# Two halves of the batches for the last experts and the last 64 steps, residuals read from PSUM by VectorE, and new operation lists in a two-layer block kernel

## What is computed

```
x = x + ga * attn0(layernorm(x) * (1 + ca) + sa)      # layer 0: gated delta rule, step by step over time
x = x + gb * ffn0(layernorm(x) * (1 + cb) + sb)       # layer 0: 8 experts, top 2, plus its own input
x = x + ga * attn1(layernorm(x) * (1 + ca) + sa)      # layer 1: state space layer, chunks of 64 steps
x = x + gb * ffn1(layernorm(x) * (1 + cb) + sb)       # layer 1: 128 -> 512, butterfly, gelu, butterfly, -> 128

def ffn0(xt):                                         # all experts computed, weighted by w
    h  = silu(einsum('nd,edh->enh', xt, we1) + be1)
    eo = einsum('enh,ehd->end', h, we2) + be2
    return xt + einsum('ne,end->nd', w, eo)           # w: softmax over the top 2 of 8 logits

def attn1(x):
    xi, w = x @ in_proj                               # xi: causal convolution of 4 taps -> xh;  A = w * w_base
    y = ssd(xh, A, chunk=64)                          # decays, running sums, state carried to the next chunk
    return y @ out_proj.T
```

## Time and profile before

| | us |
|---|---|
| median of 3 runs | 543.15 |
| lowest and highest | 539.29, 543.17 |
| the profiled execution | 537.53 |
| its span, first to last instruction | 535.6 |
| PE, ACT, DVE, POOL busy in the span | 434.6, 368.9, 329.5, 173.2 |

### The profile page before, as it was taken

How to read it: one execution, slowest core, us unless ns; L and a number is a source line. 1 busy time by engine, 2 the same in 40 slices (tenths; PEclk the granted TensorE clock), 3 DMA queues, 4 the chain that set the end, 5 groups by cost and what they waited for, 6 DMA issues and landing times.

```text
span 535.6 us, 6713 instructions
## 1 busy us (share of the span) xinstructions
PE 434.6 (81%) x2060; PEld 290.7 (54%) x2060; DVE 329.5 (62%) x741; ACT 368.9 (69%) x624; POOL 173.2 (32%) x240
## 2 busy tenths in 40 slices
PE   4767876669878688999888999999899999965075
PEld 2546845447556466567655656666566565641021
DVE  0525954786899963979989995499231194211910
ACT  5889777894966838788439774765997877925233
POOL 1150940574347761077940305233002100030001
PEclk9889997999999899999999999999999999995579
DMA  8739665024800068002074000000000000000000
GB/s 197 246 83 260 203 267 158 1 52 108 215 4 2 1 158 219 3 0 61 19 182 118 1 1 21 0 1 1 1 0 21 0 1 2 1 20 0 0 1 20
DMA packets 34323, 35.46 MB, mean 66 GB/s; under 512 B 12776, under 2 KB 30320, under 8 KB 34032
## 3 DMA queue, kind: packets, MB, share of 16 engines
q1 hardware_dynamic: 34000, 30.84, 21.9%
q10 hardware_dynamic: 288, 4.19, 2.0%
HBM read 13.78 MB, written 1.05 MB: 28 GB/s over the span
## 4 chain that ended last, share of the span: by engine, by line
PE 32%; ACT 8%; POOL 5%; DVE 4%; issue 3%; POOLq 0%; DVEq 0%
PE psS L776 9%; PE psF L761 9%; PE psM L812 3%; PE psM L819 3%; PE psB L718 2%; PE psM L596 2%; PE psB L605 1%; ACT hS L1329 1%; POOL QS L3019 1%; ACT L1286 1%; ACT hid L1479 1%; POOL A L3006 1%; PE psM L799 1%; PE psM L805 1%; ACT L1284 1%
## 5 line engine op out<-in xcount | busy, mean ns | idle before, releaser
L776 PEld LDWEIGHTS psS<-we2s,hid 128*128 128x128 f32 x1024 | 129.3, 193 | 43.7 <-issue 34.9
L761 PE MATMUL psF<-h,we1s 128*128 128x512 f32 (+1 forms) x320 | 134.8, 523 | 21.2 <-ACT hid L1479 15.3
L776 PE MATMUL psS<-we2s,hid 128*128 128x128 f32 x1024 | 131.8, 277 | 8.7 <-DVE acc L2063 5.5
L1479 ACT ACTIVATE hid<-psF,col 128x512 f32<-128x512 f32 (+1 forms) x160 | 93.1, 599 | 59.8 <-PE psF L761 51.2
L761 PEld LDWEIGHTS psF<-h,we1s 128*128 128x128 f32 x320 | 54.8, 194 | 61.7 <-ACT hid L1479 33.0
L3019 POOL TENSOR_TENSOR QS<-H,qn 128x256 f32<-128x256 f32 x64 | 51.4, 814 | 83.7 <-DVE H L2051 71.0
L2063 DVE SCALAR_TENSOR_TENSOR acc<-psS,gate,acc 128x128 f32<-128x128 f32 x128 | 40.4, 340 | 59.2 <-PE psS L776 47.8
L1286 ACT ACT_TABLE_LOAD x44 | 56.5, 1283 | 1.5 <-PEq L3326 0.7
L2030 DVE TENSOR_TENSOR psT<-wrep,H 128x360 f32<-128x360 f32 x64 | 46.1, 720 | 12.8 <-DMA wrep<-XX 11.1
L2051 DVE TENSOR_TENSOR_SCAN H<-A,psT 128x320 f32<-128x320 f32 x64 | 52.3, 817 | 1.7 <-issue 0.3
L1284 ACT ACT_TABLE_LOAD x30 | 38.5, 1283 | 0.5
(11 more groups left out here) (194 smaller groups left out, 641.8 us busy)
## 6 DMA issues: line engine op xcount, KB each, us to landing
wrep<-XX SPq DMA_DIRECT2D x72, 160.0 KB, 3.3
krep<-kn SPq DMA_DIRECT2D x64, 128.0 KB, 2.5
hid<-fold_mats_dram SPq DMA_DIRECT2D x22, 256.0 KB, 4.4
we1s<-we_dram ACTq DMA_DIRECT2D x1, 2048.0 KB, 7.8
we2s<-we_dram ACTq DMA_DIRECT2D x1, 2048.0 KB, 12.5
outT_dram<-x SPq DMA_DIRECT2D x4, 256.0 KB, 2.6
M<-mats_dram SPq DMA_DIRECT2D x1, 576.0 KB, 5.1
x<-xT_dram SPq DMA_DIRECT2D x2, 256.0 KB, 6.8
```

The lines of the kernel that those rows point to most:

```text
L761: mm(bank[name][:, 0:ncols(w)], we1s[:, e, k * P:(k + 1) * P], h2[w % 2][:, 0:ncols(w)], start=True, stop=True).then_inc(s_hid_mm, 1)
L776: last = mm(bank[name][:, t * P:(t + 1) * P], hid[n % 2][:, k, t * P:(t + 1) * P], we2s[:, e, k, :], start=(k == 0), stop=(k == HT - 1))
L1479: nc.scalar.activation(hid[x_ % 2][:, k, 0:c], psF[n % 2][:, 0:c], ACT.Silu, bias=pc("be1", HT * e + k)).then_inc(s_hid_done, 1)
```

## The change

1. The experts of the last window run as two units: `EU` lists (window, first batch, last batch), units 4 and 5 being batches 0 to 3 and 4 to 7 of window 4. `first`, `hidden`, `second`, `mix` and `experts_back` take a unit; in units 4 and 5 they work on 256 columns and two tiles of tokens.
2. The last block of 64 steps of the second layer runs as two units of four batches: `SU`, units 3 and 4. They have tiles of their own (`last4`, `hS1`, `EE1`, laid over `krep`, which the recurrence has left by then), and banks of their own for unit 4 (S0, S1, F0, F1). Their `ssd_last`, `ssd_carry`, `ssd_factors` and `ssd_state` are left out, since no block follows.
3. The residuals: DVE adds the product times the gate to x directly from PSUM, one operation of 64 (or 32) columns for each batch (`experts_residual`, `ssd_residual`, `ffn_residual`). `experts_branch`, `ssd_branch`, `ffn_out` and POOL's `ssd_residual`, `ffn_gate` and `ffn_residual` go. POOL adds the experts' own input times the gate to x (`experts_gate`, `experts_skip`) as soon as it is normalized, and the feed-forward's bias times the gate (`ffn_shift`, with `out_bias` once on DVE) after the centring.
4. The list of every engine is placed anew, SP's with it.

```diff
+EU = [(w, 0, NB) for w in range(W - 1)] + [(W - 1, 0, NB // 2), (W - 1, NB // 2, NB)]
+SU = [(v, 0, NB) for v in range(NV - 1)] + [(NV - 1, 0, NB // 2), (NV - 1, NB // 2, NB)]
+LASTS = [u for u in range(len(SU)) if SU[u][0] == NV - 1]
...
@@ sync
             spread_solved(1)
+            spread_keys(3)
             spread_keys(2)
-            spread_keys(3)
             spread_solved(2)
             spread_solved(3)
-            spread_keys(5)
             spread_keys(4)
             spread_solved(4)
             spread_solved(5)
+            spread_keys(5)
+            spread_keys(7)
             spread_keys(6)
             spread_solved(6)
-            spread_keys(7)
             spread_solved(7)
...
@@ tensor
+            def first(u, e, k):
+                w, a, b = EU[u]
+                n = HT * (EXPERTS * u + e) + k
...
+                mm(bank[name][:, 0:(b - a) * TWS[w]], we1s[:, e, k * P:(k + 1) * P], h2[w % 2][:, a * TWS[w]:b * TWS[w]], start=True,
                    stop=True).then_inc(s_hid_mm, 1)
...
+            first(5, 7, 0)
+            first(5, 7, 1)
+            variance(("ssd", 3))
+            first(5, 7, 2)
+            first(5, 7, 3)
+            second(5, 6, 0)
+            second(5, 6, 1)
+            second(5, 7, 0)
+            second(5, 7, 1)
+            experts_back(5)
+            ssd_steps(3)
+            center(("ssd", 4))
+            ssd_in(3)
+            variance(("ssd", 4))
+            fill(2)
+            ssd_steps(4)
+            ssd_in(4)
+            ssd_out(3)
+            ssd_out(4)
+            center(("ffn", 3))
+            center(("ffn", 4))
+            variance(("ffn", 3))
+            fill(25)
+            variance(("ffn", 4))
+            ffn_up(3, 0)
+            ffn_up(3, 1)
+            fill(34)
+            ffn_up(3, 2)
+            ffn_up(3, 3)
+            ffn_up(4, 0)
+            ffn_up(4, 1)
+            ffn_down(3)
+            ffn_up(4, 2)
+            ffn_up(4, 3)
+            ffn_down(4)
...
@@ scalar (the end of the list)
+            ln_scale(("ssd", 3))
+            modulate(("ssd", 3))
+            ssd_steps(3)
+            ln_square(("ssd", 4))
+            ssd_in(3)
+            ln_scale(("ssd", 4))
+            modulate(("ssd", 4))
+            ssd_steps(4)
...
+            ln_square(("ffn", 3))
+            ln_scale(("ffn", 3))
+            ln_square(("ffn", 4))
+            modulate(("ffn", 3))
+            ln_scale(("ffn", 4))
+            ffn_act(3, 0)
+            ffn_act(3, 1)
+            modulate(("ffn", 4))
+            ffn_act(3, 2)
+            ffn_act(3, 3)
             for i in range(0, 4):
+                ffn_act(4, i)
...
@@ vector
+            def experts_residual(u):
+                w, a, b = EU[u]
+                dve.wait_ge(s_yT_mm, u + 1)
+                dve.wait_ge(s_skip_done, w + 1)
+                ps = bank[back_bank(u)][:, 0:(b - a) * TWS[w]].rearrange("p (b t) -> p b t", t=TWS[w])
+                for i in range(a, b):
+                    last = v_.scalar_tensor_tensor(xw(w)[:, i, :], ps[:, i - a, :], mod[:, GB, i:i + 1], xw(w)[:, i, :], ALU.mult, ALU.add)
+                last.then_inc(s_x2_done, 1)
...
+            def ffn_residual(u):
+                _, a, b = SU[u]
+                ps = ut(bank[ssd_banks(u)[0]][:, 0:scols(u)])
+                dve.wait_ge(s_ffn_mm, u + 1)
+                dve.wait_ge(s_shift_done, u + 1)
+                for i in range(a, b):
+                    last = v_.scalar_tensor_tensor(xv(u)[:, i - a, :], ps[:, i - a, :], mod[:, 6 + GB, i:i + 1], xv(u)[:, i - a, :],
+                                                   ALU.mult, ALU.add)
+                last.then_inc(s_x4_done, 1)
...
@@ the list on vector, around the first feed-forward
             chunk_delta(4, 8)
+            ssd_halo(1)
+            ffn_residual(0)
+            experts_residual(2)
             chunk_outer(4, 8)
...
@@ gpsimd
             def experts_gate(w):
                 b_ = bt(brS[:, 0:ncols(w)])
-                pool.wait_ge(s_yf_done, w + 1)
-                g_.tensor_tensor(b_, b_, per_b(GB, 0, TWS[w]), ALU.mult).then_inc(s_yg_done, 1)
...
+                pool.wait_ge(s_ln_h, LN["moe", w] + 1)
+                if w > 0:
+                    pool.wait_ge(s_skip_done, w)
+                g_.tensor_tensor(b_, bt(h2[w % 2][:, 0:ncols(w)]), per_b(GB, 0, TWS[w]), ALU.mult).then_inc(s_yg_done, 1)
+
+            def experts_skip(w):
                 b_ = bt(brS[:, 0:ncols(w)])
                 pool.wait_ge(s_yg_done, w + 1)
-                g_.tensor_tensor(xw(w), xw(w), b_, ALU.add).then_inc(s_x2_done, 1)
...
+                g_.tensor_tensor(xw(w), xw(w), b_, ALU.add).then_inc(s_skip_done, 1)
+
+            def ffn_shift(u):
+                pool.wait_ge(s_gdb_done, 1)
+                pool.wait_ge(s_ln_c, LN["ffn", u] + 1)
+                g_.tensor_tensor(xv(u), xv(u), per_u(gdb[:, :], u), ALU.add).then_inc(s_shift_done, 1)
```

More of the change, by code:

```diff
@@ L80, in tiles, with batches, etiles, mixed @@
     return ncols(w) // P
-def mixed(w, e=0):
-    return EXPERTS * sum(tiles(i) for i in range(w)) + (e * tiles(w) if e else 0)
+def batches(u):
+    return EU[u][1:]
+def etiles(u):
+    w, a, b = EU[u]
+    return range(a * TWS[w] // P, b * TWS[w] // P)
+def mixed(u, e=0):
+    return EXPERTS * sum(len(etiles(i)) for i in range(u)) + (e * len(etiles(u)) if e else 0)
+def passes(w):
+    return sum(EU[u][0] < w for u in range(len(EU)))
+def expert_passes_for(s):
+    v, _, b = SU[s]
+    w = last_window(v)
+    return passes(w) + sum(EU[u][0] == w and EU[u][1] < b for u in range(len(EU)))
 def nrows(w):
@@ L1147, in _ @@
+            second(3, 3, 3)
+            first(3, 5, 0)
+            first(3, 5, 1)
+            attn_out(7)
+            second(3, 4, 0)
+            first(3, 5, 2)
+            for i in range(1, 4):
+                second(3, 4, i)
             first(3, 5, 3)
             first(3, 6, 0)
-            second(3, 4, 3)
+            center(("moe", 4))
             first(3, 6, 1)
-            attn_out(7)
             second(3, 5, 0)
+            variance(("moe", 4))
+            for i in range(1, 4):
+                second(3, 5, i)
@@ new lines, in _ @@
+            for i in range(1, 4):
+                ffn_up(2, i)
+            first(5, 0, 1)
+            ffn_down(2)
+            first(5, 0, 2)
+            first(5, 0, 3)
+            second(4, 7, 1)
+            first(5, 1, 0)
+            first(5, 1, 1)
+            second(5, 0, 0)
+            first(5, 1, 2)
+            first(5, 1, 3)
+            second(5, 0, 1)
+            first(5, 2, 0)
+            first(5, 2, 1)
+            second(5, 1, 0)
+            first(5, 2, 2)
+            first(5, 2, 3)
@@ L2471, in _ @@
             chunk_seed(2, 8)
-            experts_branch(0)
-            mix(1, 0, 0)
             chunk_delta(2, 8)
@@ new lines, in _ @@
+            ssd_norms(0)
+            mix(2, 5, 0)
+            ssd_total(0)
+            chunk_seed(4, 0)
+            chunk_delta(4, 0)
+            ssd_state(0)
+            for i in range(1, 4):
+                mix(2, 5, i)
+            chunk_outer(4, 0)
+            ssd_norm(0)
+            mix(2, 6, 0)
+            chunk_scan(4, 0)
+            ssd_residual(0)
+            chunk_seed(4, 1)
+            route_logits(3)
+            route_compare(3, 0)
+            chunk_delta(4, 1)
+            route_max(3)
@@ new lines, in _ @@
+            decays(2, 5)
+            decays(2, 6)
+            read_state(2, 2)
+            read_state(2, 3)
+            experts_skip(0)
+            decays(2, 7)
+            decays(2, 8)
+            experts_gate(1)
+            read_state(2, 4)
+            for i in range(9, 12):
+                decays(2, i)
+            read_state(2, 5)
+            decays(2, 12)
+            read_state(2, 6)
+            read_state(2, 7)
+            decays(2, 13)
+            decay_products(3)
+            decays(2, 14)
```

2018 lines of the change are left out of this document (1028 added, 990 removed).

## The result

| | us |
|---|---|
| before, median of 4 runs | 541.89 (539.29 to 543.17) |
| after, median of 4 runs | 498.4 (497.44 to 500.17) |
| ratio | 0.921, 95% interval 0.917 to 0.925 |
| span of the profiled execution | 496.4, against 535.6 |

The account below looks back on a forecast made before the run. PE's work and idle time were taken to bound the kernel until 476 us, then one tile walking between engines. Tail gain 20.0 less 0.9 less 5 leaves 14.1 us: 543 to 529, range 517 to 541.

Parts of the forecast that it names:

- The tail: From the last expert product's end (E) to the end, in halves A and B (four batches each): 59.3 to 39.3 us.
- The halves ahead of E: Last window's experts before E, the last expert product's end: 5 us lost to ACT (0 to 8.6), 0.9 more PE work.
- The residuals on the DVE: 104 small DVE operations come, nine branch operations go; cost taken as 0, range 0 to 6 us.
- The lists: New orders of all five engines, winning or losing PE idle time before the tail: taken as 0, 6 us either way.
- the first scan within 3 us of E: Sign: the last 64 steps' first DVE scan starts within 3 us of the last expert product's end.
- DVE busy over 90% from E+3 to E+18: Sign in the tail: DVE over 90% busy from 3 to 18 us after the last expert product's end.
- E between 479 and 486: Sign: the last expert product ends (E) between 479 and 486 us; it was 476.3 in the kernel before.
- keys(7) ahead of solved(6): SP's list: nothing lost if keys(7) may start by 258 us; each microsecond later delays the last window's chunk 0 equally.
- ACT doesn't hold PE: Rival, last window's experts: the tail's 20 us arrive, less 0.9, giving 524 us; chance 0.25.
- the first half is bound by ACT: Rival, last window: all 8.6 us of ACT waits and 6 of the recurrence show: 531 to 538.5 us; chance 0.18.
- the halves don't overlap: Rival, tail: the second half's steps run only when the first's are through; 541 us, no change; chance 0.10.
- the DVE stands where POOL stood: Rival: `ffn_residual(0)` in DVE's list waits 20 us for the first feed-forward product, delaying the recurrence: 549 us; chance 0.07.

Follow-up runs that it names:

- k3_residuals: The kernel before with the new functions (residuals out of PSUM by DVE) in its old order, nothing halved: 543.7 us, ratio 1.005.
- k2_oldfront: The kernel after, with the order of the kernel before on every engine ahead of the last window's experts: 537.6 us, ratio 0.994 to the kernel before.
- k1_whole: The kernel after without halves: new functions and new order ahead of window 4, tail in the old order: 506.9 us, ratio 0.936 to the kernel before.
- k4_order: The kernel before with its own functions, nothing halved, in the new order ahead of the last window: 516.1 us, ratio 0.952.
- r2_state_inside: The kernel after with eleven second-layer items (7 us) put ahead of the last recurrence's last chunk step in DVE's list alone: 507.2 us, ratio 0.936 to the kernel before.
- s4_last_only: The kernel before with its own functions, old order up to the last recurrence and window 3's experts, new order from there: 539.5 us, ratio 0.997.
- i1: The kernel after with eleven more fill products on PE ahead of the last 64 steps' output product: 495.4 us, ratio 0.914 to the kernel before.
- i2: The same kernel as i1, measured again beside the kernel after: 498.3 us, against 498.7 for the kernel after.

## Why the prediction was wrong, step by step

**The tail** was right: 40.9 us against 39.3 forecast. The first scan came at E+2.4 (E+2.3 forecast), the DVE's work on B ahead of its last Ln and Exp ended at E+19.1 (17.6), the two x3 stood at E+21.6 and 22.5 (20.5, 21.4), the down product ended at E+37.6 (35.4). The residual of four operations took 0.86 to 0.87 us (0.85). The 1.5 us lost in the DVE's half steps are the larger part of the 1.6. The operations themselves cost what the forecast said (6.9 for a half). But the waits for ACT were 1.5 instead of 1.0, and four operations, two of them running sums, waited for the DVE operation ahead of them, where the forecast let each start 0.1 before its end; that makes 0.9 us.

```profile
468.48 0.69 DVE L2401 TENSOR_TENSOR_SCAN krep<-krep 128x256 f32<-128x256 f32 x1 [0.20 <-DVE krep L2393]
...
471.81 0.69 DVE L2401 TENSOR_TENSOR_SCAN krep<-krep 128x256 f32<-128x256 f32 x1 [0.20 <-DVE krep L2393]
```

**The halves ahead of E** were nearly right in size and only half right in cause. The last window lasted 6.9 us longer, forecast 5.9 (5 for ACT and 0.9 of PE work). From its first to its last expert product, kernel before and then after:

```profile
388.20:476.30 88.10, 85.53 (x431) 56.27 (x429) 30.46 (x85) 68.37 (x102) 6.88 (x6) 1.00 0.02 4
```

```profile
360.50:455.50 95.00, 87.47 (x494) 67.56 (x492) 37.44 (x124) 71.18 (x134) 3.31 (x3) 1.00 0.03 6
```

PE idles 2.6 us in the first and 7.5 in the second, 4.9 more, and its own work is 1.9 more. What PE waited for in the second (us in total, times, the longest):

```profile
PE psF L844 <- ACT hid L1613: 2.9, 2, 1.6
PE psS L859 <- DVE acc L2231: 1.2, 1, 1.2
```

Two waits of 1.0 and 0.7 for ACT's normalizations and one of 1.1 for the DVE come on top. So ACT accounts for 4.6 of the 7.5 us, and for 2.1 of the 2.6 before: about half of the 4.9 is ACT's, and most of the rest is the DVE's, which the forecast had not priced here. With nothing but the halves and their lists between the two kernels, the cost is larger: the last window lasts 87.7 us in k3_residuals and 95.0 in k2_oldfront (7.4 lost), and 85.6 in k1_whole and 95.0 in the kernel after (9.4 lost). The tail goes from 55.6 to 40.9 in the first pair (14.7 won) and from 58.9 to 40.9 in the second (18.0 won). The new functions by themselves won 3.7 us of the tail in k3_residuals (59.3 to 55.6) but 0.5 in k1_whole (k4_order's 59.3 to 58.9), where PE's products ran slower: the first centring took 2.08 us against 1.36, the up products 5.48 against 4.05.

**The residuals on the DVE** were put at 0 with 0 to 6 of loss. In the old order all new functions together lose 2.1 us, and since they win 3.7 in that kernel's tail, about 6 ahead of E, the end of the range. In the new order they gain up to 4, 9 as first measured. The range had no gain in it: the step counted the DVE's time and POOL's own time, and not what stood behind the two operations on POOL, ACT and DVE.

**The lists** are the step that failed: "I take 0, with 6 either way". They gave 25, with before's functions, and 30 with the two items of POOL well placed. The forecast had the number in hand that bounds this, if PE's work stays the same: its idle time before E of 66.8 us, 46.6 of it behind the first 60. That "no row prices this" was no ground for 6: a gain of up to the 46 was open, and the fast end of the range, 517, had only 3 us of it. It also read the profile from the last half only. PE's slices stand mostly at 6 to 8 tenths up to the sixteenth, where the two kernels differ most (32.8 against 17.4 us idle). And the one sentence that saw it ("it was the order of its list that held it", of the DVE's 9.8 us) was used to cancel a cost, not priced as a gain.

Of what would show the forecast right: no POOL on the chain behind E, right; the first scan within 3 us of E, right (2.4); DVE busy over 90% from E+3 to E+18, nearly (13.13 of 15 us, 88%); E between 479 and 486, wrong (455.5).

**SP.** keys(7) ahead of solved(6) cost nothing: the 24 issues end at 261.4 and solved(6) goes at 261.84, when its data has just been written (261.81).

```profile
198.36 63.02 SPq L587 DMA_DIRECT2D krep<-kn  x24
261.84 5.47 SPq L601 DMA_DIRECT2D wrep<-XX  x8
```

**The rivals.** That ACT doesn't hold PE was wrong (2.9 us on hidden tiles). That the first half is bound by ACT had a last window 9.5 us longer, and the two pairs without other changes have 7.4 and 9.4; but only part of that is waiting for ACT, and its other 6 us, of the residuals, show in the old order alone. That the halves don't overlap was wrong (DVE, E+2.4 to E+19.1). That the DVE stands where POOL stood did not come up: `ffn_residual(0)` runs its eight operations at 302.43 in 1.62 us, with no wait, since its product is done by then. In k3_residuals, with the old order, it would have been possible; there the recurrence took 81.4 us, 1.5 more than before. No rival had the order of the lists winning more than 6.

The page "VectorE: DVE Perf Modes" of the Trainium skill (section on the TRN2 errata) speaks against tiles under 512 elements. A fixed part was paid, as the page says: 0.43 us for 256 columns against 0.68 for 512. The two pairs above show what outweighs it here: the overlap of two halves won 15 to 18 us in a tail that one tile walked alone, and 6 to 8.5 us in the whole.

## What to carry to other kernels

Where a hand-made list is replaced on every engine, the idle time of the engine that sets the time, ahead of its last product, bounds the gain there as long as that engine's work stays the same: take it by stretches, over the whole run and not only where the diff is read most easily, in profiles whose busy times agree, and keep it as an end of the range. A single wait removed from an in-order list may only pass to the next item (three repairs gave 0 to 4 us here, the lists together 25); look at what else stands between the steps of the longest serial chain, and move all of it, on all engines. And before a gain is put down to a function, ask whether the other version's items were placed as well: two items of POOL were 5 of 9 us here.

## What the runs showed of the hardware

A wait of PE can cost more than its length: after 6.04 us of standing, sixteen products took 6.16 us instead of 3.62, at a granted clock of 0.60 (r2_state_inside).

The granted clock goes with the whole time from run to run. Of 69 runs of the kernel before, the 18 with a mean clock of 0.939 or more have a median span of 537.3 us, the 19 with 0.929 or less one of 540.4. PE's busy time up to E was 409.5 us in the first profile of the kernel before and 418.9 in s4_last_only, which has the same products. PE's idle time moves the other way. In four profiles with the same lists ahead of E (the kernel after twice, i1, i2) PE is busy for 405.9 to 413.8 us up to E and idle for 44.9 to 48.6, and E lies at 454.5 to 459.0. So a few microseconds between two single profiles tell nothing, neither in a start nor in an idle time, unless PE's busy time in the stretch agrees. The kernel after ran at 0.952 to 0.969 in nine runs. The order alone did not bring that: k4_order, 25 us faster than the kernel before, ran at 0.926 to 0.939. How much of the gain is clock was not taken apart.

Eleven fill products right ahead of a wait did not secure the clock: 1.87 us after them a pair of products took 0.70 us in one profile and 1.06 in the other.
